# Attention and expert layer on one core: expert groups of two batches with sums kept in PSUM, turns written out, and 128-row bias operands

## The reference

```python
def xattn(x1, x2, memory_k, memory_v):        # 16 heads of 16
    q = x1 @ Wq + bq
    k = concat([x2 @ Wk + bk, memory_k], 1)   # 256 + 256 keys
    v = concat([x2 @ Wv + bv, memory_v], 1)
    return softmax(q k^T / 4) v @ Wp + bp

def ffn(x):                                   # E = 8, F = 1024
    router = softmax(x @ w_router); gates = softmax(x @ w_gating / 0.1)
    h = silu(x @ w_gate[e]) * (x @ w_up[e])
    cw = router * gates;  cw = cw / (sum(cw) + 1e-9)
    return sum_e cw[e] * (h @ w_down[e])      # all eight experts for every token

x = x + xattn(layernorm(x), fside_BxSxS_0, ctx_1024, ctx_1024)
x = x + ffn(layernorm(x))
```

## Time and profile before

| what | value |
|---|---|
| median of 3 runs | 3067.25 us (3063.12 to 3073.32) |
| the profiled execution's own time | 3072.85 us |
| its span, first to last instruction | 3071.1 us |
| granted TensorE clock, mean | 0.973 |
| TensorE matmul busy | 2925.6 us (95%), 25728 matmuls |
| TensorE weight load busy | 2789.9 us (91%) |
| VectorE busy | 2354.2 us (77%) |
| ScalarE busy | 1694.3 us (55%) |
| GpSimd busy | 1746.3 us (57%) |

### The profile page before, as it was taken

The page is one execution under the profiler, slowest core; times in us unless marked ns, Lnnn a source line. Parts: engine busy times, 40 slices in busy tenths (PEclk is TensorE's granted clock), DMA queues, the critical chain, the costliest instruction groups (busy, mean ns, idle before and its releaser), DMA issues.

```text
span 3071.1 us, 76767 instructions
## 1 busy us (share of the span) xinstructions
PE 2925.6 (95%) x25728; PEld 2789.9 (91%) x25728; DVE 2354.2 (77%) x5137; ACT 1694.3 (55%) x3953; POOL 1746.3 (57%) x1644
## 2 busy tenths in 40 slices
PE   5878899999999989999999989999999989999999
PEld 3656799999999989999999989999999989999998
DVE  4778778787878868878787878978887666666666
ACT  4777555555555545555555545555554434444443
POOL 3555556565656656556565656656655545454554
PEclk8989899999999999999999999999999999999999
DMA  1011212112121221212112131211212231222121
GB/s 56 22 44 33 68 51 81 49 50 88 49 84 49 77 74 50 84 50 81 49 50 88 49 107 49 61 59 56 77 55 81 63 100 53 77 56 77 55 85 52
DMA packets 199166, 195.06 MB, mean 64 GB/s; under 512 B 13288, under 2 KB 198768, under 8 KB 198768
## 3 DMA queue, kind: packets, MB, share of 16 engines
q1 hardware_dynamic: 198768, 190.00, 20.3%
HBM read 173.04 MB, written 16.91 MB: 62 GB/s over the span
## 4 chain that ended last, share of the span: by engine, by line
PE 90%; DVE 3%; issue 3%; ACT 2%; DMA 1%; SPq 1%; POOL 0%; DVEq 0%; ACTq 0%; POOLq 0%
PE ps_s L646 24%; PE ps_t L646 24%; PE ps_o L674 24%; PE ps_s L726 4%; PE ps_m L548 4%; PE ps_t L760 3%; PE ps_a L748 1%; PE ps_a L750 1%; PE ps_m L542 1%; PE ps_m L586 1%; PE ps_m L556 1%; PE ps_m L601 1%; DVE negmax L1074 0%; DVE Pt_lo L1082 0%; PE ps_m L593 0%
## 5 line engine op out<-in xcount | busy, mean ns | idle before, releaser
L1170 POOL TENSOR_TENSOR acc<-acc,wout 128x512 f32<-128x512 f32 x512 | 721.9, 1410 | 875.9 <-DVE wout L960 874.7
L774 ACT ACTIVATE h_hi<-hf 128x256 fp32r<-128x256 f32 x1024 | 424.6, 417 | 432.6 <-DVE hf L943 216.7
L674 PE MATMUL ps_o<-h_hi,wd_hi 128*128 128x256 f32 x2048 | 579.7, 283 | 1.0 <-DVE wout L960 1.0
L674 PE MATMUL ps_o<-h_hi,wd_lo 128*128 128x256 f32 x2048 | 579.6, 283 | 0.0
L674 PE MATMUL ps_o<-h_lo,wd_hi 128*128 128x256 f32 x2048 | 579.2, 283 | 0.0
L946 DVE TENSOR_TENSOR h_lo<-hf,h_hi 128x256 fp32r<-128x256 f32 x1024 | 495.8, 484 | 8.7 <-ACT h_hi L774 8.7
L939 DVE SCALAR_TENSOR_TENSOR hf<-hf,ps_s 128x256 f32<-128x256 f32 x512 | 214.8, 420 | 282.0 <-ACT hf L771 279.1
L771 ACT ACTIVATE hf<-ps_s 128x256 f32<-128x256 f32 x512 | 196.9, 385 | 394.1 <-PE ps_s L646 384.2
L939 DVE SCALAR_TENSOR_TENSOR hf<-hf,ps_t 128x256 f32<-128x256 f32 x512 | 214.5, 419 | 259.5 <-ACT hf L771 257.5
L1074 DVE TENSOR_REDUCE negmax<-ps_s 128x1 f32<-128x512 f32 x512 | 347.7, 681 | 83.6 <-PE ps_s L726 82.1
L771 ACT ACTIVATE hf<-ps_t 128x256 f32<-128x256 f32 x512 | 196.8, 384 | 385.6 <-PE ps_t L646 383.5
(11 more groups left out here) (165 smaller groups left out, 7712.9 us busy)
## 6 DMA issues: line engine op xcount, KB each, us to landing
stage_w<-in_L_ffn_w_gate_dram SPq DMA_DIRECT2D x128, 256.0 KB, 2.9
stage_w<-in_L_ffn_w_up_dram SPq DMA_DIRECT2D x128, 256.0 KB, 3.0
stage_w<-in_L_ffn_w_down_dram SPq DMA_DIRECT2D x128, 256.0 KB, 2.7
xh<-d_xh SPq DMA_DIRECT2D x64, 256.0 KB, 3.5
xl<-d_xl SPq DMA_DIRECT2D x64, 256.0 KB, 3.9
cwb<-d_cw SPq DMA_DIRECT2D x128, 128.0 KB, 3.3
X<-in_x_dram SPq DMA_DIRECT2D x32, 256.0 KB, 3.3
C<-in_fside_BxSxS_dram SPq DMA_DIRECT2D x16, 256.0 KB, 2.7
```

Source lines behind the costliest of these rows:

```text
L674: mm = pe.matmul(ps_o[:, c, :], wt[:, q, c * P:(c + 1) * P], hid[:], start=(q == 0 and c == 0 and n == 0), stop=(q == FC - 1 and c == DC - ...
L774: act.activation(h_hi[q][:], hf[q][:], ACT.Copy).then_inc(hh_done.sem, 1)
L1170: pool.tensor_tensor(part, part, wout[:], ALU.add).then_inc(acc_done.sem, 1)
```

## The change

The groups have two batches: `GB = 2`, eight groups, `LAG = 3`. Attention runs alone in turns -2 to 2, turns 3 to 16 hold both (turn 16 only the rest of attention), turns 17 and 18 the expert layer alone. There are 512 expert steps as before.

An expert step takes one chunk of 128 hidden columns and both batches of the group, 512 tokens. `gate` and `up` make 6 matmuls each with 512 columns, in a bank each (`ps_g`, `ps_u`), `down` makes 6 with 512 columns. `ps_o` is two banks, in which an expert's 8 chunks are summed by TensorE; `weigh_output` runs twice after each eighth step, and `add_output` on GpSimd for all experts but the first of a group. There is one `hf`. A unit of weights now serves two steps, so the weights are loaded and split twice as often: three loads, three roundings and three subtractions for two steps.

The misc items have one bank in the expert turns (`ps_m`). TensorE's order in a step is gate, up, down, products with the values, misc item, score, transposed score. The maximum of the scores on VectorE (`negmax`) goes to the end of the step, the reads of the products with the values come two steps earlier.

The tokens stay in SBUF (`xh[0..1]`, `xl[0..1]`, written by the x2T item), and `group_end` is gone: transposing `acc` is a misc item "y" in steps 5 and 7 of the turn after a group's last, and residuals are loaded ahead. All turns are written out. `zT_hi, zT_lo` are now the same buffers as `xT_hi, xT_lo`. `brow` and `minus_one` have 128 rows; `brow` is zeroed first, and rows 0 and 1 hold what they held.

```diff
-    GB = 4
+    GB = 2
+    PN = GB * N
...
-        brow = sb("brow", [2, 4, D], F32R)
-        minus_one = sb("minus_one", [2, P], F32R)
+        brow = sb("brow", [P, 4, D], F32R)
+        minus_one = sb("minus_one", [P, P], F32R)
...
-        ps_o = pb("ps_o", [P, DC, N])
-        ps_m = [pb(f"ps_m{i}", [P, 512]) for i in range(2)]
-        ps_gu = [ps_s[1], ps_t[1]]
+        ps_o = pb("ps_o", [P, DC, PN])
+        ps_m = pb("ps_m", [P, 512])
+        ps_g, ps_u = ps_s[1], ps_t[1]
...
+        def turns(body, before_ffn=None, first_weights=None):
+
+            for b in range(-2, LAST + 1):
+                if b == 1 and first_weights:
+                    first_weights()
+                if b == LAG and before_ffn:
+                    before_ffn()
                 body(Turn(b))
...
+            def times_tokens(ps, f, w):
+
+                n, g, q = 0, f // GROUP, f % FC
+                for tok, wt in passes((xh[g % 2], xl[g % 2]), w):
+                    for c in range(DC):
+                        mm = pe.matmul(ps[:], wt[:, c, q * P:(q + 1) * P], tok[:, c].rearrange("p k n -> p (k n)"),
+                                       start=(n == 0), stop=(n == 3 * DC - 1))
+                        n += 1
+                return mm
+
+            def gate(f):
+
+                unit = f // FC
+                if f % FC == 0:
+                    pe.wait_ge(wl_done, 3 * unit + 1)
+                if f % GROUP == 0:
+                    for count in (x2T_h, x2T_l):
+                        pe.wait_ge(count.sem, GB * (f // GROUP + 1))
+                wait_for(pe, gate_done, f)
+                times_tokens(ps_g, f, W[unit % 2]["g"]).then_inc(g_ps, 1)
+
+            def up(f):
+
+                unit = f // FC
+                if f % FC == 0:
+                    pe.wait_ge(wl_done, 3 * unit + 2)
+                wait_for(pe, hf_done, f)
+                times_tokens(ps_u, f, W[unit % 2]["u"]).then_inc(u_ps, 1)
+
+            def down(f):
+
+                unit, q, at = f // FC, f % FC, f % EXPERT
+                pe.wait_ge(hl_done, f + 1)
                 if q == 0:
+                    pe.wait_ge(wl_done, 3 * unit + 3)
                 for c in range(DC):
+                    if at == 0:
+                        wait_for(pe, wout_done, DC * (f // EXPERT - 1) + c + 1)
                     for n, (hid, wt) in enumerate(passes((h_hi[q], h_lo[q]), W[unit % 2]["d"])):
                         mm = pe.matmul(ps_o[:, c, :], wt[:, q, c * P:(c + 1) * P], hid[:],
+                                       start=(at == 0 and n == 0), stop=(at == EXPERT - 1 and n == 2))
+                    mm.then_inc(d_ps, 1)
...
             def body(turn):
                 for step in range(STEPS):
+                    f = turn.f(step)
+                    if f is not None:
+                        if f + 1 < FSTEPS:
+                            gate(f + 1)
+                            up(f + 1)
+                        down(f)
...
+            def tanh_of(f):
+
+                act.wait_ge(g_ps, f + 1)
+                wait_for(act, hl_done, f)
+                act.activation(hf[:], ps_g[:], ACT.Tanh, scale=0.5).then_inc(tanh_done, 1)
...
+            def gate_of(f):
+
+                dve.wait_ge(tanh_done, f + 1)
+                dve.scalar_tensor_tensor(out=hf[:], in0=hf[:], scalar=1.0, in1=ps_g[:],
+                                         op0=ALU.add, op1=ALU.mult).then_inc(gate_done, 1)
...
+            def weigh_output(f, c):
+
+                expert = f // EXPERT
+                g, e = expert // E, expert % E
+                dve.wait_ge(d_ps, DC * f + c + 1)
...
+                if e == 0:
+                    wait_for(dve, y_ps, GB * g)
+                    part = acc[:, c].rearrange("p k n -> p (k n)")
+                else:
+                    wait_for(dve, acc_done, ADDS * g + DC * (e - 2) + c + 1)
+                    part = wout[:, c, :]
...
+            def weights_ahead(f):
+
+                if f % FC == 0:
+                    if f // FC + 1 < UNITS:
+                        weights_low(2, f // FC + 1)
+                elif f // FC + 2 < UNITS:
+                    weights_low(0, f // FC + 2)
+                    weights_low(1, f // FC + 2)
```

More of the change, by code:

```diff
@@ L250, in has @@
             def has(self, d):
-                return self.attn and (not self.fixed or 0 <= self.b + d < B)
+                return 0 <= self.b + d < B
             def wait(self, eng, count, d, nth):
[L255 to L261, removed]
@@ L317, in released @@
                           "cwT": (cwT_done, 1)}[name]
-            return [(d, count, nth)]
+            return [(count.sem, (turn.b + d) * count.per + nth)] if turn.has(d) else []
         def misc(turn, step):
             for n, (s, name, k, d) in enumerate(MISC):
-                if s == step and any(turn.has(at) for at, _, _ in released(name, k, d)):
+                if s == step and released(turn, name, k, d):
                     return n, name, k, d
@@ L616, in do_misc @@
                     turn.wait(pe, x2T_l, -1, 1)
+                    x2_hi, x2_lo = tokens(turn.b - 1)
                     for t in range(QT):
@@ L664, in down @@
-            def down(turn, step, q):
-                unit = step // GB
-                turn.wait_ffn(pe, hl_done, FC * step + q + 1)
+                project(bank(turn, n), D, D, a, 1, w, bias).then_inc(count.sem, 1)
+            def times_tokens(ps, f, w):
+                n, g, q = 0, f // GROUP, f % FC
+                for tok, wt in passes((xh[g % 2], xl[g % 2]), w):
+                    for c in range(DC):
+                        mm = pe.matmul(ps[:], wt[:, c, q * P:(q + 1) * P], tok[:, c].rearrange("p k n -> p (k n)"),
+                                       start=(n == 0), stop=(n == 3 * DC - 1))
+                        n += 1
+                return mm
@@ L863, in body @@
+                    f = turn.f(step)
+                    if f is not None:
+                        if f + 1 < FSTEPS:
+                            tanh_of(f + 1)
+                        weights_ahead(f)
                     if step == 19 and turn.has(1):
@@ L1036, in body @@
                 for step in range(STEPS):
-                    ahead(turn, step, 0, tanh_done, gate_of)
+                    f = turn.f(step)
+                    if f is not None and f + 1 < FSTEPS:
+                        gate_of(f + 1)
                     if turn.has(-1):
@@ L1128, in body @@
                         normalise(turn, 2, X, mv, rstd, XN, xn_done)
-                    weigh_output(turn, step)
-                    ahead(turn, step, 1, hh_done, low_of)
-            turns(dve, body, None, before_ffn, group_end)
+                    d, i = item_at(step, AHEAD)
+                    if turn.has(d):
+                        turn.wait(dve, s_ps, d, i + 1)
+                        if i % 4 == 0:
+                            turn.wait(dve, mq_l, d, i // 4 - 1)
+                        dve.tensor_reduce(negmax[:, (i // 4) % 2, i % 4:i % 4 + 1], one_bank(turn, ps_s, i)[:], AX.X, ALU.max,
+                                          negate=True).then_inc(max_done.sem, 1)
+            turns(body, before_ffn)
         @block.gpsimd
```

641 lines of the change are left out of this document (266 added, 375 removed), and 2 rows, old and new, of the table MISC.

## The result

| | before | changed |
|---|---|---|
| median | 3068.35 us (4 runs) | 2842.92 us (4 runs, 2842.07 to 2845.9) |
| ratio | | 0.9267, 95% interval 0.925 to 0.9284 |
| the profiled execution's own time, span | 3072.85, 3071.1 us | 2842.41, 2840.6 us |
| matmuls, busy | 25728, 2925.6 us | 16512, 2754.5 us |
| weight loads, busy | 2789.9 us | 2248.5 us |

The change took 7.3% off; 2831 us had been forecast, 2795 to 2900 as the range.

What follows compares the result with a forecast made beforehand. TensorE's own stream was taken to bound turns with the expert layer; start 229.2, twelve mixed turns at 169.9, turns 15 to 18 and the end gave span 2834, execution 2836, less 5 for the median: 2831 us, range 2795 to 2900.

Steps and rivals of the forecast that it cites:

- start of the expert layer: Turn 1's stretch beginning at 103.7, turns 1 and 2 at 57.6 each, plus 10.3 for the start: 229.2 us.
- turns 3 to 14, each: Mixed turns of attention and expert layer: 176.8 - 5.8 (expert matmuls) - 1.6 (bias) + 0.5 (transposes) = 169.9 us.
- Bias matmuls: Padding 2-row bias matmuls to 128 rows saves 0.27 us each, six per turn, 1.6 us per mixed turn.
- Rival 4: Padding does nothing, the delay coming from the change of matmul, not the 2 rows: 2854 us; 12%.
- 512 columns: Expert matmuls: 18 of 512 columns at 0.230 replace 36 of 256 at 0.120, saving 0.18 us per step, 92 us.
- Rival 3: A 512-column matmul costs nearly two of 256, by the skill page's rule: 69 us less gained, 2900 us; 6%.
- Loops: Written out, the eight looped mixed turns (about 181.1 us) cost what turn 13 does (176.8), and group ends go.
- The cover: Work that must stay hidden behind TensorE, chiefly the chain through hf: each deadline met early by 1.3 us or more.
- the lap: Chain through the single hf from one tanh to the next: 3.3 us, against a step of 4.14 alone, 5.3 mixed.
- rivals 1 and 2: Chain through hf sets the step, near 3730 us, 4%; chain late only in heavy steps, 2898 us, 16%.
- Weights: Doubled loads, roundings and subtractions stay hidden: 5 us per slot round in 8.3 or more; ScalarE some 120 us busy.

## Why the prediction held, and where it was off

**The share of each part**, from runs: writing out 41 us, padding 40, and both 81; from there to the changed kernel with 256-column matmuls, 2985.5 to 2927.9, 58 us for the groups of two and all that came with them; then 85 us for 512 columns. Together 224, beside 225 between the medians. The 58 us are a remainder, and no run takes them apart. The traces of the two kernels at its ends say where they lie: the first matmul of `down` starts at 334.1 us in the one and at 232.7 in the other, and from there to the last one it is 45 us longer, since two more of its turns are mixed, although three drains of 13 to 14 us are gone. An ordinary mixed turn takes 174.5 and 175.0 us, so what changed within it, the sums in PSUM included, takes nothing off it.

**The sum's terms.** TensorE as the pace of turns 3 to 18 held. The sum by its stream came within 7 us, in part by errors that cancel:

| term | predicted | measured |
|---|---|---|
| start of the expert layer | 229.2 | 231.7 |
| turns 3 to 14, each | 169.9 | 169.0 to 171.0, mean 170.3 |
| turn 15 | 159.3 | 160.5 |
| turn 16 | 136.8 | 139.0 |
| turn 17 | 132.4 | 132.3 |
| turn 18 to the last matmul of `down` | 128.3 | 124.0 |
| from the last matmuls of `down` to the end | 9.5 | 9.4 |
| span | 2834 | 2840.6 |
| median less the profiled execution's own time | -5 | +0.5 |

Of the 12 us between 2831 and 2843, 5 are in the last row: the old profiled execution lay above its median, and I carried that over to the new one, where it isn't so. The other 7 are what is left of two errors: up to the end of turn 16 the stretches are 11 us longer than the sum (2.5 at the start, 5 in turns 3 to 14, 3 in turns 15 and 16), and turn 18 is 4 us shorter. Its last step has no gate and up product of a next step, 12 matmuls or 2.8 us, which the sum counted. That turn 17 came out so well is in part luck: it holds eight transposes (about 0.9 us) that I had left out, and its matmuls start 0.2275 apart and not 0.230.

**Bias matmuls.** Mechanism right, size off: 0.27 us each was counted, 0.42 measured (0.38 in the old order, where a mixed turn written out falls from 176.8 to 174.5 us). The missing part was in the earlier trace rows all along: the pair behind the bias matmul, at 1517.88, lasts 0.50 us where other pairs last 0.40. I summed two distances and the third was long too. In the mixed turns this is 2.5 us instead of 1.6, 11 us over twelve turns, which was more than made up by losses elsewhere: the two waits about step 29 (0.6 us a turn), and others that no run separates. Rival 4 (padding does nothing) is refuted by three kernels. I had left the first turns out, since other waits would take up the gain; with 2 rows the expert layer starts 9 us later, so they count as well. That makes the start of 229.2 us, so near the 231.7 measured, a matter of luck: without the padding it would have been 241, 12 us behind the sum.

**512 columns.** 92 predicted, 85 measured, with more saved in the turns alone and less in the mixed ones. Rival 3, by which only 23 us would have been gained, is refuted.

**Loops.** The mixed turns and the turns alone came out as read. Turn 2 at 57.6 did not: written out it takes 63.4 in the old kernel, and in the new the first turns take 55.6 and 60.3 us. By the end of turn 1 the kernel is 5.5 us behind the sum (turn 1's stretch begins at 106.5 and not 103.7, and takes 60.3 and not 57.6), and turn 2 with the expert layer's start gives 3 of it back (64.9, not 67.9). What makes turn 2 slow stays open.

**The cover, the step that was wrong.** "Each is early by 1.3 us or more" failed. In the changed kernel's turn 17 `gate_of` ends 0.9 us (the median) ahead of the next gate matmul and `low_of` 1.0 ahead of its first `down`; the least is 0.14 and 0.05. For these three deadlines of TensorE I wrote a clock of a step, and left out the fourth, the next tanh, which waits for this step's low part. I had only set the lap's 3.3 us beside the step's 4.14. By my own clock the low part was done at 5.0 and the next gate product ready at 4.14 + 1.5 = 5.6, so 0.6 was to spare, with 0.8 for a low part that takes 1.14 on the mean in that turn:

```profile
L916 DVE TENSOR_TENSOR h_lo<-hf,h_hi 128x512 fp32r<-128x512 f32 x32 | 36.4, 1139 | 20.0 <-ACT h_hi L742 19.7
```

The lap there is 0.60 + 0.69 + 0.69 + 0.63 + 1.14 = 3.75, with handovers (0.17, as in the kernel with one spare operation) 3.9 us in a step of 4.13. Some 0.2 us is to spare on the mean, and nothing in the 22 steps in which the tanh waited for the low part. In mixed turns VectorE's own queue has some 161 of 170 us bound. So rivals 1 and 2 weren't far off: an extra microsecond per step on VectorE was enough to end on the other side of the old time. I had judged VectorE by its busy share, which fell as predicted in direction (148 to 134 us per turn, though by 14 and not by 33: the low parts alone kept their 33.5 us, and the row of L916 from 911 to 1082), and counted neither the 20 us in which it stands in order behind ScalarE's rounding nor the time it loses to GpSimd. That the doubled weight splitting on GpSimd slows VectorE was not among the prices at all.

**Weights.** Loads, roundings and subtractions at twice the rate stayed off TensorE's path as predicted. ScalarE was busy for 105 us per mixed turn and not for 120, since tanh and high part on 512 columns take less than twice on 256, which I hadn't counted. The DMA share rose from about 0.21 to 0.30 and the flow from 64 to 90 GB/s in mixed turns.

**What stays open.** Why turns 0 and 1 are slower than before (55.6 and 60.3 us for 51.7 and 57.6), and turn 2 slower than turn 1. The granted clock differs between some of them (turn 1 takes 60.3 us at 0.89 in the changed kernel, 56.9 at 0.94 in the one with little GpSimd work), but turn 0 had 0.90 before and has 0.89 now, and no run separates the clock from the waits. Also the separate shares of the earlier start and the missing drains within the 58 us. No version tried beats the changed kernel beyond its interval: two `hf` buffers give the lap room, but TensorE sets the pace.

## What to carry to other kernels

Read the slack of an engine from its queue, not from its busy share: add to the busy time what it stands for in order behind another engine in the middle of its chain. And test a cover with one spare operation: if it costs nothing there is room; here it cost 0.57 us per step for a length of 1.05, and whatever else is added there will be paid for too. A matmul that leaves array rows unused may cost more than a full one; padding its operands with zeros is worth a try wherever such matmuls stand in a dense stream.

## What the runs showed of the hardware that was not expected

- A matmul with 2 active rows in a stream of 128-row ones lengthens three distances, by 0.09, 0.20 and 0.13 us. 2 and 64 rows cost the same (2883.5 and 2881.9 us).
- VectorE operations with two operands in SBUF wait for GpSimd's running operation: 1.18 and 1.28 us for 16 and 2 elements beside a 1.3 us subtraction on GpSimd, and 0.15 to 0.20 in the kernel where GpSimd's subtractions were short. The spare product fell from 1.05 to 0.70 us there. Operations that read PSUM kept their 0.68 us in all kernels. The Trainium skill, "SBUF — State Buffer", section "Who interferes with whom", says that a VectorE instruction with two SBUF inputs contends with a GpSimd instruction that reads SBUF, and calls such contention an exclusive lock; these rows agree with it. Operations with one tensor in SBUF aren't all free of it here: the layer norm's two TENSOR_SCALAR on 2 elements average 0.60 and 0.71 us in a mixed turn of the changed kernel, and 0.16 in the one with short subtractions.
